# Batch 0 of a gated attention and expert block: another order on ScalarE, GpSimd and one DMA queue

## The reference

```python
def _L0_xattn_ref(teacher_logits, teacher_features, Wq, bq, Wk, bk):
    query = einsum('bnc,dc->bnd', teacher_features, Wq) + bq
    key = einsum('bnc,dc->bnd', teacher_features, Wk) + bk
    energy = einsum('bnd,bmd->bnm', query, key)
    attention = softmax(energy, axis=-1)
    return einsum('bln,bmn->blm', teacher_logits, attention)

def _L0_ffn_ref(x, router_w, shared_gate, shared_up, shared_down, w_gate, w_up, w_down):
    g = flat @ shared_gate.T
    u = flat @ shared_up.T
    shared_out = sigmoid(g) * u @ shared_down.T
    weights = softmax(flat @ router_w.T, axis=-1)        # 8 experts
    top_w, top_idx = top_k(weights, 2)
    ...                                                  # bf16: he = sigmoid(ge) * ue, de = he @ wd
    return x + shared_out + routed

x = x + tanh(g_xattn[0]) * _L0_xattn_ref(layernorm(x), ctx_1024, Wq, bq, Wk, bk)
x = x + tanh(g_ffn[0]) * _L0_ffn_ref(layernorm(x), router_w, ...)
```

## Time and profile before

| | us |
|---|---|
| runs | 301.31, 300.79, 299.51 |
| median | 300.79 |
| profiled execution | 300.05 |
| its span, first to last instruction | 298.3 |
| TensorE busy (span's share) | 285.3 (96%) |
| VectorE | 190.8 (64%) |
| ScalarE | 157.6 (53%) |
| GpSimd | 144.9 (49%) |

### The profile page before, as it was taken

How to read it: one execution, slowest core, us unless ns; L and a number is a source line. 1 busy time by engine, 2 the same in 40 slices (tenths; PEclk the granted TensorE clock), 3 DMA queues, 4 the chain that set the end, 5 groups by cost and what they waited for, 6 DMA issues and landing times.

```text
span 298.3 us, 5614 instructions
## 1 busy us (share of the span) xinstructions
PE 285.3 (96%) x1569; PEld 203.6 (68%) x1583; DVE 190.8 (64%) x552; ACT 157.6 (53%) x276; POOL 144.9 (49%) x166
## 2 busy tenths in 40 slices
PE   8889999799999999989999999999999999999994
PEld 3567757578867877877888777766666666666572
DVE  0697888349954558775887489455445547777533
ACT  2690478740665852643724570256666666766700
POOL 4809850984760176096077527013443345555510
PEclk9999999999999999999999999999999999999999
DMA  7999995271008012000992995324443483764975
GB/s 236 401 286 234 224 233 107 89 266 71 0 2 282 1 55 89 0 0 8 198 235 85 156 207 165 85 72 114 132 112 108 115 275 110 230 239 142 347 267 193
DMA packets 30477, 46.02 MB, mean 154 GB/s; under 512 B 2864, under 2 KB 20016, under 8 KB 30448
## 3 DMA queue, kind: packets, MB, share of 16 engines
q1 hardware_dynamic: 19296, 26.61, 29.2%
q0 software_dynamic: 10432, 17.99, 25.8%
q10 hardware_dynamic: 720, 1.05, 1.0%
HBM read 39.58 MB, written 14.72 MB: 182 GB/s over the span
## 4 chain that ended last, share of the span: by engine, by line
PE 67%; DVE 16%; issue 8%; POOL 7%; ACT 2%; DVEq 0%; POOLq 0%; ACTq 0%
PE bank L823 16%; PE bank L540 10%; PE bank L542 10%; PE bank L541 10%; PE bank L840 8%; PE bank L813 3%; PE bank L535 2%; PE bank L831 2%; POOL xg L471 2%; DVE st L1138 2%; POOL xT_lo L436 2%; POOL hT_lo L461 1%; PE bank L554 1%; DVE probT_lo L1203 1%; PE bank L564 1%
## 5 line engine op out<-in xcount | busy, mean ns | idle before, releaser
L524 POOL DMA_INDIRECT z<-ysb,dest x39 | 42.1, 1079 | 54.5 <-ACT ysb L1110 54.2
L471 POOL DMA_INDIRECT xg<-lnb,slot x32 | 32.0, 1000 | 25.2 <-DVE slot L1274 16.5
L1473 DVE TENSOR_TENSOR hrow<-sigc,bank 128x352 bf16<-128x352 f32 x39 | 20.3, 521 | 32.6 <-ACT sigc L1100 32.6
L823 PE MATMUL bank<-wgu_lo,xTb 128*128 x156 | 36.0, 313 | 0.0
L823 PE MATMUL bank<-wgu_hi,xTb 128*128 x156 | 36.0, 313 | 0.0
L1100 ACT ACTIVATE sigc<-bank 128x352 f32<-128x352 f32 x39 | 18.1, 463 | 28.3 <-PE bank L823 28.3
L540 PE MATMUL bank<-lnT_hi,sgu_lo 128*128 128x512 f32 (+2 forms) x72 | 30.0, 417 | 1.4 <-DVE sig L1339 0.9
L840 PE MATMUL bank<-wd_sb,hTb 128*128 (+1 forms) x104 | 29.0, 381 | 0.8
L542 PE MATMUL bank<-lnT_hi,sgu_hi 128*128 128x512 f32 (+2 forms) x72 | 28.5, 395 | 0.0
L541 PE MATMUL bank<-lnT_lo,sgu_hi 128*128 128x512 f32 (+2 forms) x72 | 28.4, 394 | 0.0
L1110 ACT ACTIVATE ysb<-bank,wt 128x512 bf16<-128x512 f32 x39 | 26.8, 687 | 1.5 <-PE bank L840 1.1
(11 more groups left out here) (213 smaller groups left out, 636.4 us busy)
## 6 DMA issues: line engine op xcount, KB each, us to landing
xt<-xg SPq DMA_DIRECT2D x39, 129.0 KB
xT_raw<-xT SPq DMA_DIRECT2D x4, 1024.0 KB, 6.0
acc<-x SPq DMA_DIRECT2D x4, 1024.0 KB, 9.2
z<-z SPq DMA_DIRECT2D x6, 512.0 KB, 5.4
out<-acc SPq DMA_DIRECT2D x12, 256.0 KB
wgu_lo<-wguT POOLq DMA_DIRECT2D x2, 1408.0 KB, 15.0
wgu_hi<-wguT POOLq DMA_DIRECT2D x2, 1408.0 KB, 13.3
wd_sb<-wdT POOLq DMA_DIRECT2D x2, 1024.0 KB, 10.9
```

Source lines behind the costliest of these rows:

```text
L471: nc.gpsimd.indirect_dma_start(out=xg, out_offset=bass.IndirectOffsetOnAxis(ap=slot[:, c, j:j + 1], axis=0), in_=lnb[c][:, j, :], in_offse ...
L524: nc.gpsimd.indirect_dma_start(out=z, out_offset=bass.IndirectOffsetOnAxis(ap=dest[:, u:u + 1], axis=0), in_=ysb[:, r, :], in_offset=None) ...
L823: mm = pe.matmul(bank[2 * v + half_][:, 0:I], xTb[:, v, k, :], wgu(k, bass.ds(e, 1), half_ * I, I), start=(k == 0), stop=(k == NT - 1))
L1473: V.tensor_tensor(hrow[:, v, 0:I], sigc[:, v, :], bank[2 * v + 1][:, 0:I], ALU.mult).then_inc(s["ch"], 1)
```

## The change

Four edits, all of them of order; no instruction is added or taken away.

- ScalarE, batch 0: after `choice_exp` come gates 0 and 1, `prob_high(1, 0)` and `(1, 1)`, `hidden_high` 0 and 1, then `rows_again`, `prob_high(1, 2)` and `(1, 3)`, gate 2, the four `add_ln2`, `hidden_high` 2.
- GpSimd, batch 0: `hidden_low` 0 and 1 come ahead of `factor1(1)`.
- SyncE: the x rows of batch 2 are loaded right after the context of batch 3, ahead of the wait for the parts of x.
- TensorE, batch 2: the first chunk of `down(1, 2)` (3 products) comes ahead of `turn_ln2(2, 0)` and `(2, 1)`.

```diff
@@ -296,10 +296,12 @@
                 if b == 2:
                     sp.wait_ge(s["proj"], 6)
                     load_ctx(3)
+                    load_x(b)
                 sp.wait_ge(s["xThi"], b)
                 sp.wait_ge(s["xTlo"], b)
                 load_xT(b)
-                load_x(b)
+                if b != 2:
+                    load_x(b)
 
             sp.wait_ge(s["padout"], 16 * (E + 1))
             sp.wait_ge(s["scat"], 16 * TOP * LT * last_b)
@@ -489,10 +491,10 @@
                 if b == 0:
                     pool.wait_ge(s["placed"], TOP)
                 x_low(b + 1)
+                hidden_low(b, 0)
+                hidden_low(b, 1)
                 if b == 0:
                     factor1(1)
-                hidden_low(b, 0)
-                hidden_low(b, 1)
                 scatter(b, 0)
                 hidden_low(b, 2)
                 scatter(b, 1)
@@ -759,9 +761,10 @@
             mix(b, range(3, 4))
             down(b - 1, 0)
             down(b - 1, 1)
+            down(b - 1, 2, (0,))
             turn_ln2(b, 0)
             turn_ln2(b, 1)
-            down(b - 1, 2)
+            down(b - 1, 2, (1, 2))
             turn_ln2(b, 2)
             turn_ln2(b, 3)
             down(b - 1, 3)
@@ -1027,7 +1030,6 @@
                     for j in range(LT):
                         normalise(b + 1, j)
                     choice_exp(b)
-                    rows_again(b)
                 else:
                     soft(b + 1, 2)
                     soft(b + 1, 3)
@@ -1042,6 +1044,19 @@
                     choice_exp(b)
                 gate_shared(b, 0)
                 gate_shared(b, 1)
+                if b == 0:
+                    prob_high(1, 0)
+                    prob_high(1, 1)
+                    hidden_high(0, 0)
+                    hidden_high(0, 1)
+                    rows_again(0)
+                    prob_high(1, 2)
+                    prob_high(1, 3)
+                    gate_shared(0, 2)
+                    for j in range(LT):
+                        add_ln2(0, j)
+                    hidden_high(0, 2)
+                    continue
                 add_ln2(b, 0)
                 add_ln2(b, 1)
                 hidden_high(b, 0)
```

## The result

The changed kernel takes 296.38 us (median of 4 runs, 295.96 to 297.64), the kernel before, timed beside it, 300.15 us (4 runs, 299.35 to 301.31). The ratio is 0.9884, with a 95% interval of 0.9854 to 0.9914: 3.8 us or 1.2% faster, where 3.8 us were forecast. The forecast of 297.0 us stands 0.6 us above the measured median because it was reckoned from a median of 300.79, which one more run brought down to 300.15.

What follows compares the result with a forecast made beforehand. TensorE, busy 285.3 of 298.3 us, was taken as the bound. The terms 2.81 + 0.33 + 0.27 + 0.40 = 3.81 us took the median of 300.79 to a forecast of 297.0 us, range 295.8 to 299.2.

Steps and rivals of the forecast that it cites:

- Part 1: ScalarE's new order in batch 0 closes TensorE's holes, so mix(1) starts at 58.83 instead of 61.64: 2.81 us.
- Part 3: Batch 2's x rows load earlier, so mix(1)'s products run without late starts: 0.33 us, bounds 0 to 0.33.
- the coupling: ScalarE's order gains nothing without the earlier x load, since mix(1)'s third row would still start at 67.24.
- 0.27 us at shared_out(0, 0): VectorE, earlier at ln2, makes shared_out(0, 0) sooner, so TensorE isn't held: 0.27 us, bounds 0 to 0.27.
- part 2: GpSimd's low parts go ahead of factor1 in batch 0, scatters unmoved: nothing on TensorE, bounds -0.3 to +0.3.
- rival (a): GpSimd's scatters don't move while all else comes 3 us earlier, so TensorE waits: 298.0, at most 298.5; chance 0.15.
- Part 4: TensorE in batch 2: three products of down(1, 2) fill the wait for lnr: 0.40 us, bounds 0 to 0.76.
- Passing on: From 62 us on, the other engines and later loads follow TensorE, so the rest moves as a block.
- Rival (d): Four ScalarE scalings ahead of the last high part delay GpSimd's queue: slower, 303.3 if ScalarE stood 10 us; chance 0.04.

Runs made afterwards that it cites:

- run 2: Only the load of batch 2's x rows moved ahead, in the kernel before: 300.14 us, ratio 0.9997.
- run 6: Only TensorE's batch 2 edit (first chunk of down(1, 2) ahead of the turns), in the kernel before: 300.04 us, ratio 0.9982.
- run 7: The kernel before with two unused powers (2.2 us) added on GpSimd ahead of the factors of batch 1's second layer norm: 300.54 us, ratio 1.0016.
- run 1: Only ScalarE's new order in batch 0, in the kernel before: 300.42 us, ratio 1.0012.
- run 3: The changed kernel with the x rows of batch 2 loaded where they were before: 300.34 us, ratio 1.0007.
- Run 4: The changed kernel with GpSimd's order as before (factor1 ahead of the low parts): 296.08 us, ratio 0.9862.
- run 10: The changed kernel with GpSimd's order as before (factor1 ahead of the low parts), timed once more: 296.24 us, ratio 0.9859.
- run 8: The changed kernel with two unused powers (2.2 us) added on GpSimd ahead of batch 1's second layer norm factors: 298.4 us, ratio 0.9955.
- run 5: Only GpSimd's new order (low parts ahead of factor1), in the kernel before: 300.54 us, ratio 1.001.
- run 9: The changed kernel itself, timed again: 296.3 us, ratio 0.9878.

## Why the prediction was right

- **Part 1**, 2.81 us: 2.91 by place (10.81 - 7.90). Each step stands in the rows above: the table load behind choice_exp, the product at 51.03 followed by TensorE at 51.87, no wait ahead of the second turns, the low parts in time. No drain followed the table load (its end at 49.20, the gate at 49.22), so the doubt raised by the Trainium skill's "ScalarE: Activation LUTs", section "What ACT_TABLE_LOAD costs", isn't borne out here either.
- **Part 3**, 0.33 us by the rows coming in time: the size is right, 0.33 (24.74 - 10.81 = 13.93 to 21.50 - 7.90 = 13.60), but not all of it is the rows'. The load alone won 0.20 (run 2: 24.54 - 10.80 = 13.74). The rest is mostly the slow start of mix(1)'s own first product behind its 0.45 us hole, where the next product follows after 0.34 us and not 0.23: it is still there in run 2, and gone in the changed kernel because part 1 closed the hole. The prediction's sum for the third row, 61.64 + 24 x 0.227 + 0.1, also comes to 67.19 and not 67.1, so that row was 0.05 us late in the profile before and not 0.1. That the agreement is so close is luck too: with the x rows as late as in runs 6 and 7 the 13.93 would have been 14.13 or 14.22.
- **Part 3**, the coupling: that part 1 is worth nothing without it, which was argued from one row, was shown by runs 1 and 3; by place the price of leaving it out was even above nothing (0.6 to 0.9 us at down(0, 2) in run 1), because the clock's answer to the hole was not in the reckoning. The load landed some 13.5 us after its issue, more than the 9.45 bound of before, and still 8 us ahead of its use.
- **Part 3**, 0.27 us at shared_out(0, 0): not won (6.10 us from down(0, 0) to down(0, 2), 6.07 before). The step that failed is in part 2: "the scatters start where they did". They start half a microsecond later, because of the 0.72 us gap behind factor1, so lnr waits 0.51 us for GpSimd and shared_out with it. This is rival (a) on a small scale: GpSimd's slack was put at 0.2 us and was -0.5. Run 4, without the gap, has the 0.27 us (5.80).
- **Part 2**, nothing for TensorE, bounds -0.3 to +0.3: it costs 0.3 (runs 4 and 10), so the low bound was reached. This is the same 0.3 us as in the point above, seen from the other side.
- **Part 4**, 0.40 us: 0.40, held by shared_out(1, 1), which ends at 126.95 + 0.74 = 127.69, with down(1, 3) at 127.75.
- **Passing on**: from down(0, 2) to down(1, 1) 43.35 us before and 43.24 after, and from down(1, 3) to the end of the span 166.49 and 166.55. So what was won passed to the end as far as the trace can tell; the second figure agrees by luck to 0.06, since that stretch scatters by 0.7 us.
- Sum by place 3.61 us where 3.81 was forecast (3.6 to 4.0 with the scatter of the late load); the medians differ by 3.8, an agreement with the forecast that is partly luck, since one term of 0.27 was missing and the spread is wider than the miss. The mechanism, the range and the call (faster by over 1%) held. Rival (d), ScalarE's scalings ahead of the last high part, has that part begun at 60.53 and done at 61.14, 4.6 us before GpSimd takes it up (65.70).

## What to carry to other kernels

When an engine at 96% has a few holes, ask for each what holds the next thing behind it: closing 2.8 us of them was worth nothing until the load that gated the third row of tiles had been moved as well, and either edit timed alone would have been thrown away. After such an edit look again at the engines that had idle time: what one of them could do for nothing before (2.2 us on GpSimd) now costs its full price. Effects of some tenths of a microsecond can't be read from total times here (runs of one kernel spread over 1 to 4 us). The distance between two places in the trace shows them to a few hundredths where engines wait only for each other; a place that waits for a DMA's landing moved by 0.3 us between kernels that are the same up to it.

## What the hardware showed that I had not expected

- TensorE's granted clock fell to half after holes of 2.48 us (run 1, 0.51 over 3.3 us) and 2.93 us (run 3), behind long stretches at full use, and cost 1.5 and some 1.3 us more in the profiled executions. The mean clock was 0.994 or less in six of ten executions of run 1 and nine of ten of run 3, and 0.998 or more in the others, so the same kernel seems to go either way. The Trainium skill, "TensorE: Matmul & The Clock Gate", section "Part 1: The HAM clock gate (the "warmup" mystery)", has the clock at half when the engine has lately been idle; these traces agree as to the level. In the kernel before, holes of 0.93 and 1.34 us some three microseconds apart left it at 1.00 in the profile, and so did the single one of 1.62 us in run 8.
- The first scatter follows a GpSimd subtraction of 128x512 elements by 0.16 to 0.19 us (a merged row shows it under its first shape, 96x512), but factor1's product of 4 elements a partition by 0.72 us, in every run with that order (changed, 3, 5, 8, 9) and none of the others.
